# GpSimd takes some pieces of a convolution kernel's set-up, and one more tile uses the three-product convolution

## What is computed

```python
# x (32, 64, 1024) float32
out = conv1d(x, weight, groups=4, taps=9, pad=4)            # (32, 64, 1024)
h = out + (c @ c_weight.T)[:, :, None] + bias[None, :, None]
q = h @ Wq.T                                                # (.., 16)
gate = softmax over the top 16 of 64 scores q @ keys.T      # the others are 0
z = (h @ A.T).reshape(.., 64, 8) * gate[..., None]          # (.., 512)
y = x + (z @ B.T) * 2.0
```

## Time and profile before

| | |
|---|---|
| median of three runs | 234.32 us (233.80 to 234.78) |
| profiled execution, first to last instruction | 232.1 us |
| outside the first and last instruction | 2.2 us against the median |
| TensorE, VectorE, ScalarE, GpSimd busy | 227.8, 194.5, 99.5, 1.5 us |
| granted TensorE clock | 1.00 throughout |

### The profile page before, as it was taken

One profiled execution on the slowest core, in us unless ns is written; L12 is line 12 of the kernel. 1 busy time (PEld: TensorE's weight loads), 2 busy tenths in 40 slices (PEclk: granted clock), 3 DMA queues, 4 the chain that ended last, 5 costly groups with the idle time before them and its releaser, 6 DMA issues.

```text
span 232.1 us, 4019 instructions
## 1 busy us (share of the span) xinstructions
PE 227.8 (98%) x1381; PEld 203.3 (88%) x1381; DVE 194.5 (84%) x471; ACT 99.5 (43%) x246; POOL 1.5 (1%) x10
## 2 busy tenths in 40 slices
PE   7999999999999999999999999999999999999995
PEld 7898998898989889898998989889898989898884
DVE  2799899999999899998999899898998979847232
ACT  4997768246262352525334262532536242101000
POOL 2000000000000000000000000000000000000000
PEclk9999999999999999999999999999999999999999
DMA  6999064742744628173462825538281343554532
GB/s 199 372 406 395 25 194 127 274 133 93 211 151 104 218 82 270 60 211 144 95 235 74 252 82 148 187 88 263 67 272 69 60 169 90 186 145 130 180 135 92
DMA packets 23781, 38.79 MB, mean 167 GB/s; under 512 B 2768, under 2 KB 11856, under 8 KB 23760
## 3 DMA queue, kind: packets, MB, share of 16 engines
q1 hardware_dynamic: 23616, 38.45, 51.5%
q10 hardware_dynamic: 144, 0.08, 0.2%
HBM read 25.94 MB, written 12.58 MB: 166 GB/s over the span
## 4 chain that ended last, share of the span: by engine, by line
PE 90%; ACT 6%; DMA 2%; issue 1%; SPq 0%; DVE 0%; ACTq 0%
PE p_z L646 35%; PE p_out L684 13%; PE p_out L685 13%; PE p_out L692 13%; PE p_conv L600 10%; ACT h_c L395 3%; PE p_out L646 3%; PE p_conv L543 3%; DMA x_blk<-in_x_blocks 2%; ACT x_hi L359 1%; ACT a_hi L359 1%; PE p_z L668 1%; ACT h_hi L359 0%; PE p_z L692 0%; PE p_z L684 0%
## 5 line engine op out<-in xcount | busy, mean ns | idle before, releaser
L684 PE MATMUL p_out<-b_hi,zt_hi 128*128 128x512 f32 (+1 forms) x128 | 50.1, 392 | 0.0
L685 PE MATMUL p_out<-b_hi,zt_lo 128*128 128x512 f32 (+1 forms) x128 | 50.1, 392 | 0.0
L692 PE MATMUL p_out<-b_lo,zt_hi 128*128 128x512 f32 (+1 forms) x128 | 34.4, 391 | 0.0
L646 PE MATMUL p_z<-a_hi,h_lo 128*128 128x264 f32 x240 | 34.2, 285 | 0.0
L646 PE MATMUL p_z<-a_hi,h_hi 128*128 128x264 f32 x240 | 34.1, 285 | 0.0
L646 PE MATMUL p_z<-a_lo,h_hi 128*128 128x264 f32 x240 | 33.9, 284 | 0.0
L646 PEld LDWEIGHTS p_z<-a_hi,h_hi 128*128 128x128 f32 x240 | 32.0, 188 | 1.6 <-issue 0.4
L646 PEld LDWEIGHTS p_z<-a_hi,h_lo 128*128 128x128 f32 x240 | 31.3, 188 | 0.0
L646 PEld LDWEIGHTS p_z<-a_lo,h_hi 128*128 128x128 f32 x240 | 31.0, 188 | 0.0
L685 PEld LDWEIGHTS p_out<-b_hi,zt_lo 128*128 128x128 f32 x128 | 24.0, 188 | 5.6
L684 PEld LDWEIGHTS p_out<-b_hi,zt_hi 128*128 128x128 f32 x128 | 24.0, 188 | 5.6
(11 more groups left out here) (105 smaller groups left out, 258.1 us busy)
## 6 DMA issues: line engine op xcount, KB each, us to landing
x_nat<-in_x_rows SPq DMA_DIRECT2D x16, 512.0 KB, 5.0
out_dram<-x_nat SPq DMA_DIRECT2D x31, 256.0 KB, 3.3
x_blk<-in_x_blocks SPq DMA_DIRECT2D x14, 516.0 KB, 4.0
z_dram<-a_raw SPq DMA_DIRECT2D x64, 64.0 KB, 1.8
a_raw<-z_dram SPq DMA_DIRECT2D x16, 256.0 KB, 3.7
a_raw<-in_a_wq SPq DMA_DIRECT2D x8, 264.0 KB, 6.1
x_nat<-in_b_w SPq DMA_DIRECT2D x4, 512.0 KB, 8.6
x_blk<-in_x_blocks SPq DMA_DIRECT2D x2, 258.0 KB, 3.6
```

The source lines that it names most:

```text
L646: mm = nc.tensor.matmul(z_bank(t, b)[:, 0:HB], h[:, t % 2, r, :], a[:, r, b * HB:(b + 1) * HB], start=k == 0 and r == 0, stop=k == 2 and r ...
L684: nc.tensor.matmul(dst, zt_hi[:, t % 2, c, :], b_hi[:, c, cols], start=c == 0, stop=False)
L685: nc.tensor.matmul(dst, zt_lo[:, t % 2, c, :], b_hi[:, c, cols], start=False, stop=False)
L692: mm = nc.tensor.matmul(dst, zt_hi[:, t % 2, c, :], b_lo[:, c, start:stop], start=False, stop=c == JC - 1)
```

## The change

- `TW` is 4 instead of 5: tile 4 is convolved with `conv_sum(4)` and `conv_pair(4)` (9 matmuls) where `conv(4)` stood (12), and its rows are finished by `add_u_shared(4)` on ScalarE and `add_shared(4, ...)` on VectorE instead of `add_u(4)` alone. Its x is split over 1536 columns instead of 1032.
- GpSimd now rounds piece 6 of A, forms the two differences of tile 4's blocks, the low part of group 1's weights, and the low part of B's piece 0 in four pieces of 256 columns. VectorE and ScalarE lose these.
- ScalarE: `split_x(4)` moves behind `copy_q(1)`, and the rounding of the summed weights, `sum_w(1)`, moves up between `split_b(0)` and `split_b(1)`. VectorE: `sum_w(1)`, `split_x(4)` and `split_ws(1)` stand at new places.
- TensorE: `products_u(1)` moves ahead of `conv_first()`.

The parameters, the waits and SyncE's load:

```diff
-TW = 5
+TW = 4
...
-        A_ACT = tuple(r for r in range(R) if r not in A_DVE)
+        A_POOL = 6
+        A_ACT = tuple(r for r in range(R) if r not in A_DVE and r != A_POOL)
 
         def a_hi_done(r):
+            if r == A_POOL:
+                return s_ahp, 1
             return (s_ahd, A_DVE.index(r) + 1) if r in A_DVE else (s_ahi, A_ACT.index(r) + 1)
...
+        BP = 4
+
+        def w_lo_done(g):
+            return (s_wlop, 1) if g == 1 else (s_wlo, max(g, 1))
+
+        def b_lo_done(c):
+            return (s_blo, c) if c else (s_blop, BP)
...
-                    sp.wait_ge(s_blo, t + 1)
+                    sp.wait_ge(*b_lo_done(t))
```

On GpSimd:

```diff
+            pool.wait_ge(s_a[A_POOL], 16)
+            nc.gpsimd.tensor_copy(a_hi[:, A_POOL, :], a_raw[:, A_POOL, :]).then_inc(s_ahp, 1)
+
+            def split_w(g):
+                pool.wait_ge(s_whi, g + 1)
+                nc.gpsimd.tensor_tensor(w_lo[:, g % 2], w_raw[:, g], w_hi[:, g % 2].bitcast(F32), ALU.subtract).then_inc(s_wlop, 1)
+
+            def split_b(c, piece):
+                cols = slice(piece * L // BP, (piece + 1) * L // BP)
+                pool.wait_ge(s_bhi, c + 1)
+                nc.gpsimd.tensor_tensor(b_lo[:, c, cols], b_raw[:, c, cols], b_hi[:, c, cols].bitcast(F32),
+                                        ALU.subtract).then_inc(s_blop, 1)
+
+            def differ(t, ab):
+                if ab == 0:
+                    pool.wait_ge(*x_come(t))
+                blocks = x_blk[:, t % XB]
+                nc.gpsimd.tensor_tensor(blocks[:, XS + ab * XO:XS + (ab + 1) * XO], blocks[:, ab * NN:ab * NN + XO],
+                                        blocks[:, XE:XS], ALU.subtract).then_inc(s_xdp, 1)
+
+            differ(TW, 0)
+            differ(TW, 1)
+            split_w(1)
+            for piece in range(BP):
+                split_b(0, piece)
```

On ScalarE:

```diff
-                if t >= TW:
-                    act.wait_ge(s_xd, 2 * (t - TW + 1))
+                if t == TW:
+                    act.wait_ge(s_xdp, 2)
+                if t > TW:
+                    act.wait_ge(s_xd, 2 * (t - TW))
...
             split_h(2)
-            split_x(4)
             split_keys()
             take_q(1)
             split_w(1)
             copy_q(1)
+            split_x(4)
             split_b(0)
+            sum_w(1)
             split_b(1)
             take_q(2)
             exp(1)
...
             split_b(3)
-            add_u(4)
+            add_u_shared(4)
             exp(2)
-            sum_w(1)
             split_x(5)
```

On TensorE:

```diff
                     direct(0, 0, ab, 0, True, False)
-                products_u(1)
                 pe.wait_ge(*x_lo_done(0, 0))
...
             products_u(0)
+            products_u(1)
             conv_first()
...
             scores(2)
-            conv(4)
+            conv_sum(4)
+            conv_pair(4)
             out_high(0, 0)
```

On VectorE:

```diff
             split_h(2)
-            split_x(4)
             turn_h(3, 0)
             turn_h(3, 1)
-            split_w(1)
+            sum_w(1)
             copy_scores(1)
             top_first(1)
-            split_b(0)
+            split_x(4)
             take_first(1)
             top_second(1)
+            split_ws(1)
             split_b(1)
             take_second(1)
             weigh(1)
...
             gate(2)
-            sum_w(1)
             differ(5, 0)
             differ(5, 1)
-            split_ws(1)
             turn_z(2)
+            add_shared(4, 0)
+            add_shared(4, 1)
             turn_h(4, 0)
             turn_h(4, 1)
             split_x(5)
```

More of the change, by code:

```diff
@@ L147, in adaln_ffn @@
         s_wlo = sem("s_wlo")
+        s_wlop = sem("s_wlop")
+        s_blop = sem("s_blop")
         s_xhi = sem("s_xhi")
@@ L150, in adaln_ffn @@
         s_xd = sem("s_xd")
+        s_xdp = sem("s_xdp")
         s_ws = sem("s_ws")
@@ L179, in adaln_ffn @@
         s_ahd = sem("s_ahd")
+        s_ahp = sem("s_ahp")
         s_qtp = sem("s_qtp")
@@ L589, in conv_direct @@
                     if k == 2 and t == TG:
-                        pe.wait_ge(s_wlo, 2)
+                        pe.wait_ge(*w_lo_done(1))
                     for ab in range(2):
@@ L608, in conv_sum @@
                     pe.wait_ge(s_whi, g + 1)
-                    pe.wait_ge(s_wlo, g + 1)
+                    pe.wait_ge(*w_lo_done(g))
                 pe.wait_ge(s_xhi, x_split_count(t))
@@ L690, in out_low @@
                     if t == 0 and k == 0:
-                        pe.wait_ge(s_blo, c + 1)
+                        pe.wait_ge(*b_lo_done(c))
                     mm = nc.tensor.matmul(dst, zt_hi[:, t % 2, c, :], b_lo[:, c, start:stop], start=False, stop=c == JC - 1)
```

## The result

The changed kernel takes 235.77 us (median of 5 runs, 235.04 to 235.88) against 234.32 us: ratio 1.0058, 95% interval 1.0035 to 1.0082. It is slower by 1.45 us. The profiled spans differ by more, 234.0 against 232.1 us: the spans of single executions of the kernel before lie mostly between 231.7 and 232.9, and the profiled one lies toward the low end. So what follows compares distances inside a trace, not absolute times.

The account below looks back on a forecast made before the run. VectorE was taken as the bound from 31.81 to 44.41 us, making TensorE's z stage 0.38 us later, with the other terms at 0: 234.32 + 0.38 = 234.7 us. Own case 234.1 to 235.4, whole range 233.7 to 236.6.

Parts of the forecast that it names:

- rival A: GpSimd instructions reading SBUF block VectorE's subtractions, 33.6 to 37.5 us: 1.1, plus 0.2 at A; 236.0 us; chance 0.35.
- The bound: From 31.81 to 44.41 us VectorE, running without a gap, is the bound; TensorE only 0.15 us better off.
- PE, tile 4: Nine matmuls replace twelve on TensorE, saving 0.70 us, which is spent waiting for VectorE's zt_lo(0).
- ACT, rounding of A: One of six pieces goes to GpSimd: h_c ready 0.54 us earlier, TensorE goes on at 19.86, 0.45 earlier.
- DVE's stretch: From copy_scores(1) to gate(2), work sums to +0.83 us; with the 0.45 earlier start, gate(2) ends 0.38 later.
- POOL beside DVE: VectorE's loss while GpSimd works: unknown, between 0 and 1.8 us, taken as 0.
- DVE behind gate(2): VectorE 1.2 us late after gate(2); margins at x_lo(5), add(0, 0), gate(3) of 0.8, 0.2, 1.4; cost 0, bound 0.3.
- ACT's wait at turn_q(2): TensorE reaches turn_q(2) at 33.66 and waits for ScalarE until about 34.35, giving back 0.69 us.
- The median: The span's difference, +0.38 us, is put on the measured median 234.32; 2.2 us lie outside first and last instruction.

Follow-up runs that it names:

- the last version: Rearranged nine-product kernel with GpSimd held by waits to windows, changed to split b_lo(0) into three pieces (384, 320, 320 columns) instead of four: 233.65 us, ratio 0.9970.

## Why the prediction was right or wrong

The direction was right (slower), and 235.77 lies in the stated range, 233.7 to 236.6. But the forecast 234.7 was 1.1 us short, and the time is outside the 234.1 to 235.4 that the forecast gave to its own case, and over the 235.49 from which it spoke of slower, with a chance of 0.37: what happened was rival A (0.35), not the forecast (0.50). The range holds the time only because it was drawn wide enough for A. By its steps:

- *The bound.* Right: DVE's stretch from copy_scores(1) to gate(2) sets the third z stage. gate(2) ends at 44.92 + 0.88 = 45.80, PE starts 0.14 behind it, as forecast.
- *PE, tile 4.* Right: nine matmuls, 36.26 to about 38.5, and the saving is spent waiting for zt_lo(0): 1.21 us.
- *ACT, rounding of A.* The 0.45 at 20 us was counted as a gain that moves everything; it hardly came: DVE's cast of piece 5 took 0.86 and PE waited 0.29 for piece 7, DVE's other cast, and the first convolution ended 0.16 later than in the trace before. That end varies from run to run (8.14 to 9.14 in the traces here, with products_u(1) at either place). The forecast had taken the copy for covered (it was ready at 14.81, by 15.2 as said) and asked only who waits for it, not whom it stops; rival A gave that 0.2, and DVE's cast lost 0.44. copy_scores(1) started at 31.77 instead of 31.36.
- *DVE's stretch.* The added and removed work was right: with zeros in b_lo(0), which lifts the blocking, the distance is 13.40, 0.80 over the kernel before, where the sum had 0.83.
- *POOL beside DVE.* **The step that failed.** The forecast took 0, because a_lo rows kept 698 to 701 ns beside other engines. None of these engines was POOL, so the rows said nothing about it, and the 0 had no ground. Measured: 0.55 at b_lo(1) and 0.22 at weigh(1), together 0.77, against 1.1 in rival A; its order of events (ws_lo all but free, then b_lo(1), then weigh(1), then gate(1) free) is what the rows show. The rule of the Trainium skill (SBUF — State Buffer, Who interferes with whom) is that a VectorE instruction with two SBUF inputs contends with a GpSimd instruction that reads SBUF, and that whichever issues first blocks the other for its whole length. The traces here agree with it: 1.26 us for a 0.23 us instruction that met a 1.30 us one. It deserved more than the 0.35 it got.
- *DVE behind gate(2).* Three deadlines were checked, with margins of 0.8, 0.2 and 1.4 us, and none was missed; the fourth was not looked at. DVE's q_t for scores(4) ended 0.47 us ahead of PE in the kernel before; with DVE 0.8 us later relative to PE, PE lost 0.45. The run with tile 5's differences on GpSimd shows it.
- *ACT's wait at turn_q(2).* Right in kind: PE waits from 34.1 to 34.5 for q_w near 34.3, some 0.4 instead of 0.69, the difference being the 0.45 that PE was not early. It costs nothing, as said.
- *The median.* 0.38 + 0.77 (blocking) + 0.45 (scores(4)) + 0.4 (the gain that did not come) is 2.0, and in the two traces the fifth z stage starts 1.98 later (73.97 - 71.99). The medians differ by 1.45, since the profiled execution of before is a short one. The 2.2 us that the forecast puts outside the instructions holds some 0.4 of that: within one execution of the changed kernel it is 1.8 (235.81 against 234.0).

## What to carry to other kernels

Work given to GpSimd is not free for VectorE even where GpSimd idles. List the VectorE instructions with two SBUF inputs that each GpSimd instruction meets, and count for each what is left of the GpSimd instruction when it starts; in these traces that was the price, less 0.13 to 0.15 us. Put the work where VectorE transposes or gates from PSUM, which kept their lengths beside GpSimd here (0.71 and 0.88 us), with a wait if need be. When one engine becomes later, list every later consumer of it up to where its idle time wins the delay back, small ones like a query transpose too. And a saving on the busiest engine is worth nothing where another engine already releases it.

## What was not expected of the hardware

- GpSimd's MEMSET of 1024 columns, four of them in 4.18 us, does not disturb VectorE at all; a copy and a subtraction do. Unblocked, a subtraction on GpSimd took 0.47 us for 128 columns, 0.73 to 0.75 for 256, 1.01 for 384 and 1.28 to 1.32 for 512, against VectorE's 0.38 for 256.
- The blocking works both ways: GpSimd's 256-column piece took up to 1.73 us beside VectorE, its copy of 528 columns 0.68 to 1.02 in the eight runs that have it. The copy always started while VectorE's a_lo ran, which kept its 0.70 in the changed kernel.
- VectorE's cast of 528 columns, with one input, was held up as well (0.86 instead of 0.42), while its transposes, which also read one SBUF input, kept their length beside the differences of tile 4 (0.69 and 0.71) and beside the pieces of b_lo(0) (0.71 at 36.44 in the last version).
